# A routed feed-forward kernel: expert tiles begun in slot 32 instead of 30, and three switch points tied to the end of the layer work

## What is computed

```python
y = jax.nn.gelu(x @ W.T + fc_bias + z + b)            # z: rank-16 term, b: cond, per sequence
prob = softmax(y @ w_router + b_router)
_, idx = top_k(prob, 4)                               # of 16 experts
h = relu(einsum('nd,ebd->neb', y, w1b) + b1b)         # hidden block of 128 per expert
out = x + einsum('neb,ebd,ne->nd', h, w2b, mask) + b2
```

## Time and profile before

| | before |
|---|---|
| median of 3 runs | 1100.2 us (1098.62 to 1101.34) |
| the profiled execution, its own time | 1100.98 us |
| its span | 1099.1 us |
| TensorE matmul busy | 850.5 us, 77% |
| VectorE busy | 825.7 us, 75% |
| ScalarE busy | 578.6 us, 53% |
| GpSimd busy | 576.5 us, 52% |
| DMA | 354.82 MB, mean 323 GB/s |

### The profile page before, as it was taken

How to read it: one execution, slowest core, us unless ns; L and a number is a source line. 1 busy time by engine, 2 the same in 40 slices (tenths; PEclk the granted TensorE clock), 3 DMA queues, 4 the chain that set the end, 5 groups by cost and what they waited for, 6 DMA issues and landing times.

```text
span 1099.1 us, 18009 instructions
## 1 busy us (share of the span) xinstructions
PE 850.5 (77%) x4924; PEld 677.5 (62%) x4924; DVE 825.7 (75%) x1964; ACT 578.6 (53%) x1061; POOL 576.5 (52%) x591
## 2 busy tenths in 40 slices
PE   8999998999999999999998989999999900000000
PEld 6777776778777777777776667888888700000000
DVE  4565557777676777768678987789998679888787
ACT  5565565766676676667666776767676600000000
POOL 1377777676666666666667777555555620000000
PEclk9999999999999999999999999999999955555555
DMA  6699789999898998989789999799876689999999
GB/s 185 221 364 344 264 288 371 305 326 309 292 330 298 307 311 309 314 304 324 269 295 341 325 326 319 280 337 335 296 273 230 221 351 418 425 433 429 427 429 387
DMA packets 103234, 354.82 MB, mean 323 GB/s; under 512 B 29961, under 2 KB 29961, under 8 KB 92384
## 3 DMA queue, kind: packets, MB, share of 16 engines
q1 hardware_dynamic: 59104, 217.21, 56.9%
q0 software_dynamic: 43936, 136.37, 31.5%
q10 hardware_dynamic: 96, 0.10, 0.0%
HBM read 200.47 MB, written 169.65 MB: 337 GB/s over the span
## 4 chain that ended last, share of the span: by engine, by line
PE 60%; DMA 15%; DVE 7%; ACT 7%; issue 6%; POOL 3%; ACTq 2%; POOLq 0%; SPq 0%; DVEq 0%
PE lay L1097 13%; PE hid L1205 12%; PE yps L1236 12%; DMA w2l<-yt 11%; PE trn L1190 7%; PE hid L1210 6%; PE trn L1118 3%; PE hid L1083 3%; DVE stx L960 2%; POOL xg L495 2%; ACT gsb L601 2%; DMA outT<-ys 2%; PE lay L1236 2%; PE rps L1133 1%; ACTq L612 1%
## 5 line engine op out<-in xcount | busy, mean ns | idle before, releaser
L521 POOL DMA_INDIRECT yt<-ys,ids x218 | 229.1, 1051 | 137.3 <-ACT ys L660 79.9
L495 POOL DMA_INDIRECT xg<-grow,ix x224 | 223.2, 996 | 108.5 <-issue 64.3
L769 DVE TENSOR_TENSOR gsb<-trn,gsb 128x512 fp32r<-128x512 f32 x239 | 161.1, 687 | 116.9 <-ACT gsb L601 116.1
L1097 PE MATMUL lay<-w2l,xs 128*128 128x512 f32 x768 | 191.0, 398 | 0.0
L1097 PEld LDWEIGHTS lay<-w2l,xs 128*128 128x128 f32 x768 | 142.4, 190 | 29.8
L601 ACT ACTIVATE gsb<-trn 128x512 fp32r<-128x512 f32 x239 | 142.6, 597 | 14.1 <-PE trn L1190 13.5
L1190 PE MATMUL trn<-idf,gr 128*128 128x128 f32 x956 | 144.8, 274 | 4.5 <-DVE gsb L769 4.2
L1190 PEld LDWEIGHTS trn<-idf,gr 128*128 128x128 f32 x956 | 115.1, 140 | 40.5 <-DVE gsb L769 14.7
L1205 PE MATMUL hid<-gsb,w1c 128*128 128x512 f32 (+1 forms) x576 | 127.9, 364 | 0.0
L1236 PE MATMUL yps<-w2c,hh 128*128 128x512 f32 x336 | 119.9, 438 | 6.9 <-issue 5.8
L629 ACT ACTIVATE hv<-hid,b1c 128x512 f32<-128x512 f32 (+1 forms) x94 | 52.7, 584 | 134.6 <-PE hid L1210 133.7
(11 more groups left out here) (206 smaller groups left out, 1647.3 us busy)
## 6 DMA issues: line engine op xcount, KB each, us to landing
gr<-xg SPq DMA_DIRECT2D x49, 1056.0 KB
xs<-yt SPq DMA_DIRECT2D x16, 2048.0 KB, 19.5
w2l<-yt SPq DMA_DIRECT2D x15, 2048.0 KB, 19.6
gr<-xg SPq DMA_DIRECT2D x45, 528.0 KB
stx<-xT SPq DMA_DIRECT2D x64, 256.0 KB, 3.9
outT<-ys SPq DMA_DIRECT2D x31, 512.0 KB, 20.4
xg<-xrow SPq DMA_DIRECT2D x16, 528.0 KB, 6.5
w2f<-xrow SPq DMA_DIRECT2D x16, 512.0 KB, 13.4
```

Source lines behind the costliest of these rows:

```text
L495: pool.indirect_dma_start(out=xg, out_offset=bass.IndirectOffsetOnAxis(ap=ix[:, row_buffer(b), q, k:k + 1], axis=0), in_=grows[row_buffer( ...
L521: pool.indirect_dma_start(out=yt, out_offset=bass.IndirectOffsetOnAxis(ap=ids[:, j % 8, c:c + 1], axis=0), in_=yss[result_buffer(j)][:, c, ...
L769: dve.tensor_tensor(gsb[:, :, LO, c * P:(c + 1) * P], turned[TURN_BANK[n]][:, :].rearrange("p (k t) -> p k t", k=KC), gsb[:, :, HI, c * P: ...
L1097: pe.matmul(lay[s % 2][:, :], xs[:, b % 2, k, h, cols], wls[:, k, a, :], start=(k == 0 and a == HI and h == HI), stop=False)
```

## The change

`LAG` becomes 32, and `PRE`, `LATE` and `MORE` are written as slots from which LAG is taken: 74, 64, and 67, 71, 83. The layer work stays in its slots; every step of every tile comes two slots later. `PRE` falls from tile 46 to 42, `LATE` from 36 to 32, `MORE` from 39, 43, 55 to 35, 39, 51, so by slot each of these points comes two slots earlier than before.

```diff
-LAG = 30
+LAG = 32
...
-PRE = 46
-LATE = 36
-MORE = 39, 43, 55
+PRE = SLOTS + 10 - LAG
+LATE = SLOTS - LAG
+MORE = SLOTS + 3 - LAG, SLOTS + 7 - LAG, SLOTS + 19 - LAG
```

## The result

Median 1116.67 us over six runs (1113.96 to 1119.21), before 1100.09 over six (1098.62 to 1103.06). The ratio is 1.0135, 95% interval 1.0116 to 1.0153: **slower by 14.9 us, 12.8 to 16.8**, by this ratio; the two medians by themselves are 16.6 us apart. The profiled execution took 1113.96 with a span of 1112.2, 13.1 more than the span before; it is the fastest of the six.

A forecast was written before the change was run, and what follows sets the result against it. TensorE's time and idle gaps bound it to about 880 us, then DMA; with layer work alone GpSimd is slower than TensorE. 14.1 us lost in the tail less 3.0 gained by slot 34: 11.1 slower, 1111.3 us, range 1105 to 1116.

The forecast's parts named there:

- Steps 1 and 2: Slot 32 begins at 166.0; TensorE idle 12.7 us until block 24's scatter lands; slot 34's ffn1 at 208.3, 3.0 us ahead.
- step 3: Before tile 1: TensorE's idle gap of 2.77 us goes, already inside the 3.0 us counted by slot.
- step 4: Slots 34 to 73: the same work stands in each slot and TensorE fills them, so cost nothing.
- step 7: `LATE` and `MORE`: more buffers two slots earlier bring nothing, as no result waits for its buffer in slots 64 to 76.
- step 6: `PRE`: second weights unsplit behind slot 74, so seven slots at 7.76 take 54.3, 14.1 us more than before instead of 15.5.
- The faster case: Rival: block 24 has landed by 171.1, so no stall in slot 32; 4.2 us faster, 1096; 7 in 100.
- The longer chain: Rival: gelu of blocks 33 to 35 waits for GpSimd too, or a slot 72 result for its buffer; 1117; 8 in 100.

The follow-up runs named there:

- the hold-up: The changed kernel with four more small indirect DMAs on GpSimd (5.0 us in all) directly ahead of block 24's scatter: 1115.1 us in one execution, before 1102.03.
- the reordered kernel: The changed kernel with block 24 scattered ahead of blocks 22 and 23: 1111.35 us median, ratio 1.0093; 0.9987 and 0.9986 in sessions of the 1300 us kind.
- the runs with LAG alone: The kernel before with LAG = 32 and the three points left at 46, 36 and 39, 43, 55: ratios 0.9976 and 0.9975, in 1300 us sessions.

## Why the prediction was right, and where it was short

**Right: what bounds, and the mechanism.** GpSimd falls behind TensorE while there is only layer work, and one landing pins slot 32. Steps 1 and 2 hold step by step: slot 32 began at 166.58 (forecast 166.0), TensorE got to the second turn at 175.5 (174.7), gelu of block 32 ran at 186.31 released by the DMA of xg (186.35), TensorE went on at 187.45 (187.45) and reached slot 33's ffn1 at 196.22 (196.5) and slot 34's at 207.93 (208.3). The gap was 11.90 where 12.7 stood. That gelu came out right to 0.04 us is luck: the issue came 0.4 sooner than forecast and the landing 0.4 later. That the landing is about 6 us behind the issue was taken from the median of the earlier trace rows; it held because the DMA engines were as full as before (shares of 1.02 and 1.00 at 180 to 185 us), and in the hold-up, where the share was 0.43, it was 2.7. The forecast named GpSimd's list alone and not this backlog.

**Right: step 3, step 4 and step 7.** The gap of 2.77 us before tile 1 is gone (0.75 us at 165.51 is the longest around it), slots 34 to 73 differ by 0.5 us (by 0.7 and 1.0 the other way in the hold-up and the reordered kernel), and no result waits for a buffer between slots 64 and 76.

The wait for the landing ends at 186.31, while the row at 180.05 ends at 181.01. The Trainium skill (Perfetto Trace Analysis, section DMA Instruction — SWDGE (GPSIMD)) has such a row end with the writing of the descriptors and not with the data, and this trace agrees.

**Mis-sized: step 6.** I took slots 74 and 75 as long, 8.45 us each, because of the split of the second weights, and 7.76 for slots 76 to 78 as slots without it; slot 76 of the kernel before still has it (its split stands at 676.29, and it takes 7.60). After the change slot 74 takes 8.82, slot 75 7.89 and slot 76 8.04, and with the split kept up to slot 78 (the runs with LAG alone) the sum of the seven is the same within 0.2 us. Slots 75 to 78 take 7.6 to 8.1 with the split there, 7.6 to 8.0 without it in the changed kernel. So the split does not make slot 74 long; what does was not looked for. Seven slots took 55.35 and not 54.3: 1.1 us of the difference between 11.1 and 13.1.

**Not in the sum.** 1.1 us lies among the half-size tiles. Short waits of ffn2 for ScalarE's results are scattered there, 4.0 us in all for those through `ys`; the hold-up and the reordered kernel have 3.0 and 3.2 of them and 173.68 and 173.69 us in that stretch, as before, so this is that execution's own. 0.6 us lies behind the last ffn1, and it is there in those two as well (227.3 and 227.4 against 226.6); its cause was not looked for.

**Open: the rest.** The ratio says 14.9 us, the two medians 16.6, the two spans 13.1. By the ratio the loss is inside my bounds of 5.0 to 15.3, near their upper end; the median of 1116.67 itself is 0.7 over my upper end of 1116. The traces account for the 13.1 and not for what lies above. The profiled execution is the fastest of the six of the changed kernel, the other five are 1.3 to 5.3 us longer, while before has the whole spread of 4.4 us over six. A landing that comes later in some executions would do it (the scatters of 100 to 200 us took between 2.7 and 8.1 us to land before), but no trace of a longer execution is there to show it.

**The rivals.** The faster case needed block 24 landed by 171.1; it landed 15 us later. The longer chain did not come in the profiled execution: gelu of block 33 was released by TensorE.

```profile
195.41 0.60 ACT L584 ACTIVATE grow<-lay 128x512 f32<-128x512 f32 x1 [1.68 <-PE lay L1102]
```

Its 1117 is nonetheless nearer to the median than my 1111.3, and for the longer executions, which have no trace, it is not excluded. It did come as soon as block 24 was moved ahead, one slot on. Among the tiles the clock fell once, as forecast, and no second time: it is granted at 1.00 from 195 us to the last ffn1.

## What to carry to other kernels

Read an engine's pace stage by stage: GpSimd was busy 52% of the span and still the slower engine for the first 180 us. A start that is moved later only lets the faster engine run into it sooner. Look at the transfers too: what a slow list issues lands later still when other loads fill the DMA engines (6.3 us behind its issue and not 2.7 here). When work is shifted by a number of slots, look for the wait in the unshifted list that was just covered before (here a scatter issued at 180.45 and needed at 187.63), and count what takes its place. Moving one item ahead in a queue that is too slow moves the stall to the next item.

## What the runs showed of the hardware that was not expected

The landing of an indirect DMA goes with what the DMA engines have in front of them: 2.7 us from issue behind four short ones, at a DMA share of 0.43, 5.4 to 6.6 at a share of 1.02, 7.7 for block 25 in the reordered kernel. GpSimd's own 1.27 us per DMA did not change.

The same program took 1100 us in some sessions and 1300 in others, also on one and the same chip, with layer batches of 30.5 us instead of 19.6 and waits that no event of the trace explains. LAG = 32, which with the points costs 1.35% in the one, costs nothing that can be measured in the other without them.
